# Two GpSimd additions of 128x2048 per feed-forward group, written as four of 128x512 each

## The chip, the cores and the metric

The kernel runs on one core of one Trainium2 chip. The metric is the device time of one launch in microseconds (us), the median over several runs. A core has five engines with queues of their own: PE (TensorE, matmuls), DVE (VectorE), ACT (ScalarE), POOL (GpSimd) and SP (SyncE, which here only issues transfers). They meet through semaphores and through tiles in the on-chip memory (SBUF) and in the accumulation banks of PE (PSUM).

## The reference

```python
def _L0_xattn_ref(embeds, patch_embeds, patch_lens, W_in, b_in, g_res, g_init):
    h = rmsnorm(embeds, g_res)
    h = jnp.einsum('bld,ed->ble', h, W_in) + b_in
    h_patch = rmsnorm(patch_embeds, g_init)
    return _hnet_depool(h, h_patch, patch_lens)   # a linear scan over the context, rows of it gathered, + h

def _L0_ffn_ref(x, w1, b1, w2, b2):
    h = jax.nn.gelu(jnp.einsum('bse,eh->bsh', x, w1) + b1, approximate=False)
    return jnp.einsum('bsh,he->bse', h, w2) + b2

x = x + _L0_xattn_ref(_layernorm(x, axis=-1), ctx_2048, mask_BxS2_if0, ...)
x = x + _L0_ffn_ref(_layernorm(x, axis=-1), L0_ffn_w1, L0_ffn_b1, L0_ffn_w2, L0_ffn_b2)
```

x is 4096 x 512 in float32, the context 3202 x 1024, the feed-forward layer 512 to 2048 to 512.

## The kernel before

There are two stages. The first (to about 185 us) takes x in 32 tiles of 128 rows: layer norm, projection by W_in, residual, and the result is stored to a DRAM buffer `x1_dram` (`x_part` in the profile). Beside it the context is scanned in blocks, and the scanned rows go to a DRAM table (`scan_table`).

The second stage is the feed-forward layer, in 8 groups of 512 rows, g = 0 to 7. A group is 16 steps m (`M`), each a slice of 128 hidden columns. Every float32 operand of a matmul is split into a high and a low part, so each product is three matmuls (`split_product`, L773 to L775). For each m:

- `ffn1(g, m)` on PE: 12 matmuls from `xt_hi`/`xt_lo` and the first weights into bank `h_bank[m % 2]`.
- ACT takes the gelu of it twice: `h_hi` (L734), rounded, and `g_f32` (L736), full. There is one `g_f32`, so L736 of step m waits until DVE has read that of step m - 1 (`h_split`).
- DVE makes `h_lo` as `g_f32 - h_hi` (L1134), both inputs in SBUF.
- `ffn2(g, m)` on PE: 12 matmuls from `h_hi`/`h_lo` and the second weights into the four banks `acc`. It waits for `h_lo` of its step.

PE's order within a group is ffn1(0), ffn1(1), ffn2(0), ffn1(2), ffn2(1), ... , ffn1(15), two transposes of the next group's rows, ffn2(14), the other two, ffn2(15). So at the start of a group two ffn1 stand one behind the other, with no ffn2 between ffn1(1) and the first ffn2 that needs an `h_lo` of this group. In groups 0 to 3 PE also does the scan's `carry`, three matmuls at m = 11.

What GpSimd does in a group is written out in its own `group(g, scan, prep)` (L574 on), in this order:

1. `x_cur = x_next + b2` (L579), one operation of 128x2048. It waits for the normalised rows (`n_b_ready`) and for the four stores of the previous group's output (`out_stored`), since `x_cur` is the buffer that is stored. `x_cur_ready` lets SP load the next group's rows to `x_next`.
2. Only in groups 0 to 3: `context_scale` and four `times_g_init` of 128x512 (L502) for the scan; in group 0 also four `low_weights` of 128x512 (L475).
3. `prepare(g + 1)` (L509): the gather's indices (L487), `x_next += b_in` (L491), one operation of 128x2048 in place, and then four gathers (L496), one per tile of 128x512, which add rows of the scan table to `x_next` by an indirect DMA. `step(...)` makes each operation end before the next one of the engine starts.
4. `group_scale(g + 1)` (L506, L507), which waits for DVE's statistics.

DVE waits for each tile's gather (`gathered[i]`) in `second_stats`: tiles 0 and 1 behind its step m = 11, tiles 2 and 3 behind m = 12. At the group's end it adds `acc` to `x_cur` tile by tile (L1158, waits for `x_cur_ready`), and SP stores each tile.

DVE's L1134 and its wait:

```python
dve.wait_ge(gelu_done, CREDIT + M * g + m + 1)
dve.wait_ge(h_used, NT + M * g + m - 1)
dve.tensor_tensor(h_lo[:, m % 2, :], g_f32[:], h_hi[:, m % 2, :].bitcast(F32),
                  ALU.subtract).then_inc(h_split, 1)
```

Of the kernel before, what the change touches and what calls it, by code (L numbers as in the profile page):

```python
# [22 lines left out]
ALU = mybir.AluOpType  # L23
# [7 lines left out]
P = 128  # L31
S, D, HID = 4096, 512, 2048
CTX, DG = 3202, 1024
TI = 4
# [13 lines left out]
NB = 7  # L48
NA = 3
# [4 lines left out]
STORED = 16  # L54
# [13 lines left out]
def wait_apart(engine, sem, value):  # L68

    engine.wait_ge(sem, value)  # L70
    engine.nop(nofuse=True)
# [24 lines left out]
def xattn_ffn(nc, x, ctx, mask, w_in, b_in, g_res, g_init, w1, b1, w2, b2, out):  # L96
# [11 lines left out]
    with es:  # L108
        def sb(name, shape, dt=F32):
            return es.enter_context(nc.sbuf_tensor(name, shape, dt))  # L110

        def sem(name):
            return es.enter_context(nc.semaphore(name))
# [8 lines left out]
        def place(name, shape, dt=F32, size=0, offset=None):  # L122
            where = at[0] if offset is None else offset
            t = nc.alloc_sbuf_tensor_at(name, shape, dt, offset=where)
            if offset is None:
                at[0] += size
            return t
# [12 lines left out]
        x_cur = place("x_cur", [P, TI, D], F32, 8 * KB)  # L140
        x_next_at = at[0]
        x_next = place("x_next", [P, TI, D], F32, 8 * KB)
# [32 lines left out]
        b_in_b = sb("b_in_b", [P, D])  # L175
        b2_b = sb("b2_b", [P, D])
# [64 lines left out]
        table_stored = sem("table_stored")  # L241
# [40 lines left out]
        x_cur_ready = sem("x_cur_ready")  # L282
# [147 lines left out]
        def _(pool):  # L430
            own = Tally(pool_self)

            def step(ins):
                wait_apart(pool, pool_self, own.inc(ins))
# [36 lines left out]
            def low_weights(c, q, high_ready, done):  # L471

                pool.wait_ge(w_hi_done, high_ready)
                r = slice(q * D, (q + 1) * D)
                pool.tensor_tensor(w_lo[:, c, r], w_raw[:, c, r], w_hi[:, c, r].bitcast(F32),  # L475
                                   ALU.subtract).then_inc(done, 1)

            def context_scale(b):
                pool.wait_ge(sq_done, R * b + R)
                step(pool.tensor_tensor(ss[:], ss_h[:], ss_l[:], ALU.add))  # L480
                step(pool.tensor_scalar(ss[:], ss[:], 1.0 / DG, RMS_EPS, ALU.mult, ALU.add))
                step(pool.tensor_tensor(rc[:], ss[:], neg_half[:], ALU.pow))
                pool.tensor_scalar(rc[:], rc[:], B_COEF, 1.0, ALU.mult, ALU.mult).then_inc(rc_ready, 1)

            def gather_indices(g):

                step(pool.tensor_copy(idx[:], plug[:, bass.ds(TI * g, TI)]))  # L487

            def add_bias(v, b):

                step(pool.tensor_tensor(v, v, b, ALU.add))  # L491

            def add_context(g, i, blocks):

                rows = table[0:STEP * blocks, :]
                pool.indirect_dma_start(x_next[:, i, :], None, rows, bass.IndirectOffsetOnAxis(  # L496
                    ap=idx[:, i:i + 1].bitcast(U32), axis=0), compute_op=ALU.add).then_inc(gathered[i], 16)

            def times_g_init(b, j):

                pool.wait_ge(sq_done, R * b + j + 1)
                pool.tensor_tensor(cl[:, j, :], cl[:, j, :], g_init_b[:], ALU.mult).then_inc(g_scaled, 1)  # L502

            def group_scale(g):
                wait_apart(pool, mv_b_ready, TI * (g + 1))
                step(pool.tensor_scalar(va_b[:], mv_b[:, :, 1], LN_EPS, 1.0, ALU.add, ALU.mult))  # L506
                pool.tensor_tensor(rb[:], va_b[:], neg_half[:], ALU.pow).then_inc(rb_ready, 1)  # L507

            def prepare(g, blocks):  # L509
                gather_indices(g)  # L510
                pool.wait_ge(x_next_loaded, 16 * (g + 1))
                add_bias(x_next[:], b_in_b[:].unsqueeze(1).to_broadcast([P, TI, D]))
                wait_apart(pool, table_stored, STORED + 16 * blocks)
                for i in range(TI):
                    add_context(g, i, blocks)

            def span(h, last=False):
# [56 lines left out]
            def group(g, scan, prep):  # L574

                pool.wait_ge(n_b_ready, TI * (g + 1))
                if not isinstance(g, int) or g > 0:
                    pool.wait_ge(out_stored, 16 * TI * g)
                pool.tensor_tensor(x_cur[:], x_next[:], b2_b[:].unsqueeze(1).to_broadcast([P, TI, D]),  # L579
                                   ALU.add).then_inc(x_cur_ready, 1)  # L580
                if scan:
                    context_scale(NA + g)
                    for j in range(R):
                        times_g_init(NA + g, j)
                if isinstance(g, int) and g == 0:
                    for q in range(4):
                        low_weights(7, q, 7, w2_ready)
                if prep:
                    prepare(g + 1, g + 3 if scan else NB)
                    group_scale(g + 1)  # L590

            for g in range(NB - NA):
                group(g, True, True)
            with pool.Fori(NB - NA, NG - 1) as g:
                own.looped(g, NB - NA, 1 + 1 + 1)
                group(g, False, True)
            own.left(NG - 1 - (NB - NA))
            group(NG - 1, False, False)


# [593 lines left out]
```

## Time and profile before

| | |
|---|---|
| median of 3 runs | 949.41 us |
| lowest and highest run | 947.39 and 951.27 us |
| profiled execution, span from first to last instruction | 946.3 us (the profile lists no other time for this execution) |
| PE busy | 863.1 us, 91% |
| DVE, ACT, POOL busy | 337.7, 293.1, 271.9 us |
| mean granted TensorE clock | 0.949 of full speed |
| share of PE in the chain that ended last | 77% |

The span is of one execution, the median of others. Start times in the rows below count from the span's start. A granted clock of 1.00 is TensorE's 2.4 GHz level, 0.50 its 1.2 GHz level; a window with a value between them held both.

### The profile page before, as it was taken

What the parts mean: (1) busy time and instruction counts of PE and PEld (TensorE: products, weight loads), DVE (VectorE), ACT (ScalarE), POOL (GpSimd) and SP (SyncE); (2) the same over time, 40 slices, a digit from 0 to 9 for tenths busy, and PEclk for the clock granted to TensorE, in tenths of its full rate; (3) what the DMA queues carried; (4) which work ended last, traced back from release to release, by engine and by line L of the source; (5) the groups of instructions that cost most, each with busy time, mean ns of one, the idle gap of its engine ahead of it and who ended that gap; (6) DMA issues with size and microseconds to landing.
All of it is one profiled execution on the core that took longest, in us unless ns stands there. A gap on an engine that the chain in (4) does not pass through costs nothing.

```text
span 946.3 us, 11247 instructions
## 1 busy us (share of the span) xinstructions
PE 863.1 (91%) x3781; PEld 705.7 (75%) x3781; DVE 337.7 (36%) x531; ACT 293.1 (31%) x505; POOL 271.9 (29%) x278
## 2 busy tenths in 40 slices
PE   5789786299999999899989998999899989998998
PEld 4567565178888887788868886888688868886886
DVE  4767566411452244224422442123212421242112
ACT  3465661133323422242324231222122222222221
POOL 4265455563601521043114306000600060001000
PEclk8899897689999999899999998999899989998999
DMA  7956655330314033203230223001300130000001
GB/s 224 290 176 227 226 179 144 90 136 23 45 63 147 11 48 111 95 11 44 101 108 11 44 87 81 10 1 45 79 10 0 43 77 13 0 30 15 1 1 44
DMA packets 34413, 73.13 MB, mean 77 GB/s; under 512 B 5548, under 2 KB 6572, under 8 KB 31984
## 3 DMA queue, kind: packets, MB, share of 16 engines
q1 hardware_dynamic: 25124, 57.34, 17.9%
q0 software_dynamic: 4608, 8.39, 5.9%
q10 hardware_dynamic: 4656, 7.09, 2.4%
q8 instruction: 13, 0.21, 0.1%
q14 instruction: 12, 0.10, 0.0%
HBM read 48.92 MB, written 23.89 MB: 77 GB/s over the span
## 4 chain that ended last, share of the span: by engine, by line
PE 77%; DMA 8%; DVE 7%; POOL 3%; issue 2%; ACT 1%; ACTq 1%; SPq 0%; POOLq 0%; DVEq 0%
PE acc L773 13%; PE acc L775 13%; PE acc L774 13%; PE h_bank L773 12%; PE h_bank L774 12%; PE h_bank L775 12%; DMA x_part<-xb 4%; DVE h_lo L1134 3%; PE t_bank L817 1%; DMA x_next<-scan_table,idx 1%; DMA x_next<-x_part 1%; DMA g_init_b<-in_L_xattn_g_init_dram 1%; DMA xa<-in_x_dram 1%; DVE h_lo L917 1%; POOL x_next L491 1%
## 5 line engine op out<-in xcount | busy, mean ns | idle before, releaser
L1134 DVE TENSOR_TENSOR h_lo<-g_f,h_hi 128x512 fp32r<-128x512 f32 x128 | 129.1, 1009 | 515.4 <-ACT g_f L736 507.1
L734 ACT ACTIVATE h_hi<-h_bank,b_c 128x512 fp32r<-128x512 f32 x128 | 88.3, 690 | 510.4 <-PE h_bank L775 510.4
L773 PE MATMUL acc<-w_hi,h_hi 128*128 128x512 f32 x512 | 206.7, 404 | 22.1 <-DVE h_lo L1134 22.1
L775 PE MATMUL acc<-w_hi,h_lo 128*128 128x512 f32 x512 | 204.7, 400 | 0.0
L774 PE MATMUL acc<-w_lo,h_hi 128*128 128x512 f32 x512 | 204.5, 399 | 0.0
L773 PE MATMUL h_bank<-xt_hi,w_hi 128*128 128x512 f32 x512 | 201.5, 394 | 1.5 <-DVE xt_lo L1058 1.5
L774 PE MATMUL h_bank<-xt_lo,w_hi 128*128 128x512 f32 x512 | 200.6, 392 | 0.0
L775 PE MATMUL h_bank<-xt_hi,w_lo 128*128 128x512 f32 x512 | 200.2, 391 | 0.0
L773 PEld LDWEIGHTS acc<-w_hi,h_hi 128*128 128x128 f32 x512 | 98.9, 193 | 45.4 <-issue 20.9
L775 PEld LDWEIGHTS acc<-w_hi,h_lo 128*128 128x128 f32 x512 | 99.2, 194 | 21.4
L773 PEld LDWEIGHTS h_bank<-xt_hi,w_hi 128*128 128x128 f32 x512 | 97.6, 191 | 22.5 <-ACT xt_hi L720 1.9
L774 PEld LDWEIGHTS acc<-w_lo,h_hi 128*128 128x128 f32 x512 | 99.4, 194 | 20.0
L774 PEld LDWEIGHTS h_bank<-xt_lo,w_hi 128*128 128x128 f32 x512 | 97.4, 190 | 20.5
L775 PEld LDWEIGHTS h_bank<-xt_hi,w_lo 128*128 128x128 f32 x512 | 97.1, 190 | 20.5
L736 ACT ACTIVATE g_f<-h_bank,b_c 128x512 f32<-128x512 f32 x128 | 87.3, 682 | 16.3 <-DVE h_lo L1134 16.3
L579 POOL TENSOR_TENSOR x_cur<-x_next,b_b 128x2048 f32<-128x2048 f32 x8 | 36.9, 4615 | 144.9 <-DMA out_dram<-x_cur 144.7
L773 PE MATMUL acc<-win_hi,h_hi 128*128 128x512 f32 x128 | 58.0, 453 | 13.3 <-DVE h_lo L917 13.3
L506 POOL TENSOR_SCALAR va_b<-mv_b 128x4 f32<-128x4 f32 x8 | 1.6, 197 | 216.5 <-DVE mv_b L1044 216.5
L496 POOL DMA_INDIRECT x_next<-scan_table,idx x32 | 53.6, 1674 | 15.5 <-POOL x_next L491 9.1
L775 PE MATMUL acc<-win_hi,h_lo 128*128 128x512 f32 x128 | 54.7, 427 | 0.0
L774 PE MATMUL acc<-win_lo,h_hi 128*128 128x512 f32 x128 | 54.4, 425 | 0.0
L491 POOL TENSOR_TENSOR x_next<-x_next,b_in_b 128x2048 f32<-128x2048 f32 (+1 forms) x11 | 38.0, 3452 | 21.6 <-DMA x_next<-x_part 21.0
(133 smaller groups left out, 686.5 us busy)
## 6 DMA issues: line engine op xcount, KB each, us to landing
xa<-in_x_dram SPq DMA_DIRECT2D x32, 256.0 KB, 5.8
x_part<-xb SPq DMA_DIRECT2D x32, 256.0 KB, 3.6
x_next<-x_part SPq DMA_DIRECT2D x8, 1024.0 KB, 5.1
out_dram<-x_cur SPq DMA_DIRECT2D x32, 256.0 KB, 2.1
w_raw<-in_L_ffn_w_dram ACTq DMA_DIRECT2D x6, 1024.0 KB, 11.0
cl<-in_ctx_dram SPq DMA_DIRECT2D x6, 1024.0 KB
ch<-in_ctx_dram SPq DMA_DIRECT2D x16, 256.0 KB, 2.7
scan_table<-cl SPq DMA_DIRECT2D x4, 992.0 KB
```

The source lines that it names most:

```text
L491: step(pool.tensor_tensor(v, v, b, ALU.add))
L496: pool.indirect_dma_start(x_next[:, i, :], None, rows, bass.IndirectOffsetOnAxis(ap=idx[:, i:i + 1].bitcast(U32), axis=0), compute_op=ALU. ...
L506: step(pool.tensor_scalar(va_b[:], mv_b[:, :, 1], LN_EPS, 1.0, ALU.add, ALU.mult))
L579: pool.tensor_tensor(x_cur[:], x_next[:], b2_b[:].unsqueeze(1).to_broadcast([P, TI, D]), ALU.add).then_inc(x_cur_ready, 1)
L734: act.activation(h_hi[:, m % 2, :], h_bank[m % 2][:], ACT.Gelu, bias=b1_c[:, m:m + 1])
L736: act.activation(g_f32[:], h_bank[m % 2][:], ACT.Gelu, bias=b1_c[:, m:m + 1]).then_inc(gelu_done, 1)
L773: nc.tensor.matmul(dst, a_hi, b_hi, start=first, stop=False)
L774: nc.tensor.matmul(dst, a_hi, b_lo, start=False, stop=False)
L775: return nc.tensor.matmul(dst, a_lo, b_hi, start=False, stop=final)
L817: ins = nc.tensor.transpose(t_bank[i % 2][:, k * P:(k + 1) * P], n_rows[:, i, k * P:(k + 1) * P], ident[:])
L917: dve.tensor_tensor(h_lo[:, t % 2, :], t_bank[t % 2][:], h_hi[:, t % 2, :].bitcast(F32), ALU.subtract).then_inc(t_lo, 1)
L1134: dve.tensor_tensor(h_lo[:, m % 2, :], g_f32[:], h_hi[:, m % 2, :].bitcast(F32), ALU.subtract).then_inc(h_split, 1)
```

## The change

Both 128x2048 additions of GpSimd's group are written as loops over the four tiles of 128x512. In `prepare` the gather of each tile now follows that tile's own piece of the addition; the wait for the scan table stands behind the first piece. The four pieces of `x_cur` follow one another with no wait between them, and the last one raises `x_cur_ready`. The count of the engine's own semaphore per loop turn goes from 3 to 6.

```diff
             def prepare(g, blocks):
                 gather_indices(g)
                 pool.wait_ge(x_next_loaded, 16 * (g + 1))
-                add_bias(x_next[:], b_in_b[:].unsqueeze(1).to_broadcast([P, TI, D]))
-                wait_apart(pool, table_stored, STORED + 16 * blocks)
                 for i in range(TI):
+                    add_bias(x_next[:, i, :], b_in_b[:])
+                    if i == 0:
+                        wait_apart(pool, table_stored, STORED + 16 * blocks)
                     add_context(g, i, blocks)
...
                 if not isinstance(g, int) or g > 0:
                     pool.wait_ge(out_stored, 16 * TI * g)
-                pool.tensor_tensor(x_cur[:], x_next[:], b2_b[:].unsqueeze(1).to_broadcast([P, TI, D]),
-                                   ALU.add).then_inc(x_cur_ready, 1)
+                for i in range(TI):
+                    ins = pool.tensor_tensor(x_cur[:, i, :], x_next[:, i, :], b2_b[:], ALU.add)
+                ins.then_inc(x_cur_ready, 1)
...
-                own.looped(g, NB - NA, 1 + 1 + 1)
+                own.looped(g, NB - NA, 1 + TI + 1)
```

GpSimd's order from group 0's `prepare` to the `x_cur` addition of group 1, with what each waits for, before:

```order
L487 COPY idx<-plug 128x4
L491 TENSOR_TENSOR x_next<-x_next,b_in_b 128x2048 [waits pool_self,x_next_loaded]
L496 DMA x_next<-scan_table,idx 128x512 [waits pool_self,table_stored]
L496 DMA x_next<-scan_table,idx 128x512 x3
L506 TENSOR_SCALAR va_b<-mv_b 128x4 [waits mv_b_ready]
L507 TENSOR_TENSOR rb<-va_b,neg_half 128x4 [waits pool_self]
L579 TENSOR_TENSOR x_cur<-x_next,b_b 128x2048 [waits out_stored,n_b_ready]
L480 TENSOR_TENSOR ss<-ss_h,ss_l 128x4 [waits sq_done]
```

The same place with the change (the `x_cur` addition is L581 there):

```order
L491 TENSOR_TENSOR x_next<-x_next,b_in_b 128x512 [waits pool_self,x_next_loaded]
L496 DMA x_next<-scan_table,idx 128x512 [waits pool_self,table_stored]
L491 TENSOR_TENSOR x_next<-x_next,b_in_b 128x512
L496 DMA x_next<-scan_table,idx 128x512 [waits pool_self]
...
L506 TENSOR_SCALAR va_b<-mv_b 128x4 [waits mv_b_ready]
L507 TENSOR_TENSOR rb<-va_b,neg_half 128x4 [waits pool_self]
L581 TENSOR_TENSOR x_cur<-x_next,b_b 128x512 [waits out_stored,n_b_ready]
L581 TENSOR_TENSOR x_cur<-x_next,b_b 128x512 x3
L480 TENSOR_TENSOR ss<-ss_h,ss_l 128x4 [waits sq_done]
```

Nothing else moved past the addition of `x_cur`: one operation became four with the waits in front of the first. In `prepare` the gathers of tiles 0 to 2 moved ahead of the later pieces of the addition, and each gather now waits for its piece. The other engines' orders are unchanged.

## Rows read from the trace of the kernel before

**Rows 1.** Page, 40 equal slices of the span, the granted TensorE clock in tenths.

```profile
PEclk8899897689999999899999998999899989998999
```

**Rows 2.** Page, the chain that ended last, shares of the span by engine.

```profile
PE 77%; DMA 8%; DVE 7%; POOL 3%; issue 2%; ACT 1%; ACTq 1%; SPq 0%; POOLq 0%; DVEq 0%
```

**Rows 3.** Page, costliest groups: busy and mean ns, then idle before and releaser.

```profile
L1134 DVE TENSOR_TENSOR h_lo<-g_f,h_hi 128x512 fp32r<-128x512 f32 x128 | 129.1, 1009 | 515.4 <-ACT g_f L736 507.1
```

**Rows 4.** Waits of PE from 190 us on: us in total, times, longest.

```profile
PE acc L773 <- DVE h_lo L1134: 22.1, 6, 3.8
```

**Rows 5.** Timeline of 374 to 383 us: start, duration, engine, line, operation, [idle before].

```profile
375.78 4.53 POOL L579 TENSOR_TENSOR x_cur<-x_next,b_b 128x2048 f32<-128x2048 f32 x1 [19.63 <-DMA out_dram<-x_cur]
...
376.06 4.79 DVE L1134 TENSOR_TENSOR h_lo<-g_f,h_hi 128x512 fp32r<-128x512 f32 x1 [3.06 <-ACT g_f L736]
...
376.66 0.39 PE L774 MATMUL h_bank<-xt_lo,w_hi 128*128 128x512 f32 x1
376.89 0.39 PE L775 MATMUL h_bank<-xt_hi,w_lo 128*128 128x512 f32 x1
381.10 0.77 PE L773 MATMUL acc<-w_hi,h_hi 128*128 128x512 f32 x1 [3.83 <-DVE h_lo L1134]
381.67 0.63 PE L774 MATMUL acc<-w_lo,h_hi 128*128 128x512 f32 x1
382.09 0.63 PE L775 MATMUL acc<-w_hi,h_lo 128*128 128x512 f32 x1
```

**Rows 6.** Windows of 4 us around it: busy per engine (count), granted clock, DMA, GB/s.

```profile
372.00:376.00 4.00, 4.00 (x20) 3.30 (x19) 1.01 (x2) 1.27 (x2) 0.22 (x1) 1.00 0.76 271
...
380.00:384.00 4.00, 2.90 (x7) 2.36 (x8) 1.55 (x2) 0.69 (x1) 0.31 (x1) 0.50 0.92 334
384.00:388.00 4.00, 4.00 (x14) 3.18 (x13) 0.00 (x0) 0.00 (x0) 0.00 (x0) 0.69 0.18 76
```

**Rows 7.** Chain that ended last: each group's first transposes of the next rows.

```profile
274.99 0.87 PE t_bank L817 x8
...
364.58 0.88 PE t_bank L817 x8
...
842.14 0.87 PE t_bank L817 x8
```

**Rows 8.** Timeline of 286 to 293 us, the one boundary without a PE wait.

```profile
287.00 4.63 POOL L579 TENSOR_TENSOR x_cur<-x_next,b_b 128x2048 f32<-128x2048 f32 x1 [20.43 <-DMA out_dram<-x_cur]
286.46 0.69 DVE L1134 TENSOR_TENSOR h_lo<-g_f,h_hi 128x512 fp32r<-128x512 f32 x1 [3.05 <-ACT g_f L736]
```

**Rows 9.** Timelines around 236 and 185 us: GpSimd's 128x512 pieces and L1134 among them.

```profile
235.76 2.54 POOL L475 TENSOR_TENSOR w_lo<-w_raw,w_hi 128x512 fp32r<-128x512 f32 x2
...
237.70 1.14 DVE L1134 TENSOR_TENSOR h_lo<-g_f,h_hi 128x512 fp32r<-128x512 f32 x1 [4.30 <-ACT g_f L736]
...
230.31 5.49 POOL L502 TENSOR_TENSOR cl<-cl,g_init_b 128x512 f32<-128x512 f32 x4
...
185.88 11.16 POOL L475 TENSOR_TENSOR w_lo<-w_raw,w_hi 128x512 fp32r<-128x512 f32 x9
```

**Rows 10.** PE in the first stage: a gap, and the window of 4 us around it.

```profile
81.78 0.50 PE L773 MATMUL acc<-win_hi,h_hi 128*128 128x512 f32 x1 [1.14 <-DVE h_lo L917]
...
80.00:84.00 4.00, 2.86 (x14) 2.24 (x15) 3.86 (x8) 1.75 (x5) 1.02 (x4) 1.00 0.59 130
```

**Rows 11.** Chain at 158 us, timelines of group 0, and the gathers' time to landing.

```profile
158.25 1.25 POOL x_next L491
...
161.91 1.34 POOL x_next L491
...
241.53 4.60 POOL L491 TENSOR_TENSOR x_next<-x_next,b_in_b 128x2048 f32<-128x2048 f32 x1
...
263.18 0.68 DVE L1043 BATCH_NORM_STATS2 st_b<-x_next 128x6 f32<-128x512 f32 x1
...
DMA to landing us min/median/max: 4.6/5.2/12.5
```

## Prediction, made before the changed kernel was run

> **What bounds the kernel now.** I read the page first, then the waits of PE, then the timeline of one group boundary. The chain that ended last is three quarters PE [rows 2], so time is gained only where PE stands still or runs slowly. PE's granted clock dips at regular distances all through the feed-forward stage [rows 1], about once per group. A steady matmul load should not do that, so something stops PE at each boundary. The mean of 1009 ns for DVE's L1134 [rows 3] is the second sign: undisturbed the operation takes 0.69 us [rows 8], so a few must be very long. PE's waits name the place: six waits, 22.1 us together, all for `h_lo` [rows 4].
>
> The timeline shows one of the six [rows 5]. GpSimd starts its 128x2048 addition at 375.78. DVE starts `h_lo` of the group's first step at 376.06, 0.28 us later, and ends at 380.85, which is 0.54 us after GpSimd's end at 380.31. DVE did not run slowly: it stood behind the other operation and then did its own. PE's last matmul of ffn1(1) started at 376.89; the next one starts at 381.10 after 3.83 us idle, 0.25 us behind the end of `h_lo`. Boundary 0 to 1 is the counterproof [rows 8]: there `h_lo` starts at 286.46, before GpSimd at 287.00, takes 0.69 us, and PE does not wait.
>
> The stall has a second price. PE's clock is 1.00 before it, 0.50 in the 4 us with and behind it, 0.69 in the next [rows 6]: the engine had been idle, the clock fell from its 2.4 GHz to its 1.2 GHz level, and the matmuls follow at a distance of 0.42 us instead of 0.23 [rows 5].
>
> **What a boundary costs in all.** From 274.99 to 364.58 is one group without a wait, 89.59 us [rows 7]. It contains the scan's three carry matmuls, 3 x 0.23 = 0.68 us, so a group without the scan should take 88.91. From 364.58 to 842.14 are five groups, two with and three without the scan: 477.56 us, against 2 x 89.59 + 3 x 88.91 = 445.91. The excess is 31.65 us, 6.33 per boundary. Six boundaries: 38.0 us. Of it 22.1 is the wait [rows 4] and 15.9 the slow clock, 2.65 per boundary; twelve matmuls 0.2 us later each give 2.4, which fits.
>
> **The change part by part.**
>
> *The addition to `x_cur`, four pieces.* What decides is whether DVE gets its turn between two pieces. The trace has the nearest case already: GpSimd's runs of 128x512 operations, L502 and L475 [rows 9]. Two pieces from 235.76 end at 238.30. L1134 starts among them at 237.70 and ends at 238.84, again 0.54 us behind the end of the piece that it met, while two further pieces stand behind. So DVE waits for one piece, not for the run. A piece takes 11.16 / 9 = 1.24 us in an almost free run. Bounds: 4.53 / 4 = 1.13 from below, 5.49 / 4 = 1.37 from above, where a DVE operation is in the run [rows 5, 9]. I take 1.24, the row of most pieces. At the boundary shown, `h_lo` then ends at 375.78 + 1.24 + 0.54 = 377.56 and PE starts 0.25 later, at 377.81, instead of 381.10: 3.29 us earlier. It still waits 3.83 - 3.29 = 0.54. Over six boundaries the wait goes from 22.1 to 22.1 - 6 x 3.29 = 2.4 us, gain 19.7; with 1.13 or 1.37 a piece it is 20.4 or 18.9. If a race is won as in boundary 0 to 1 the rest goes too.
>
> *The clock.* A gap of about half a microsecond stands in place of 3.8. The trace shows a longer gap that cost nothing: 1.14 us in front of 81.78, in a window where PE was busy 2.86 of 4 us; its clock is 1.00 [rows 10]. So I take the 15.9 us as gained in full, lower end of the gain 0.
>
> *The later steps of a boundary.* `h_lo` of the second step comes while pieces 3 and 4 run. It is late by one piece at most, 1.24 + 0.54 - 0.69 = 1.1 us. From there on an ffn2 stands between two ffn1, 12 x 0.23 = 2.7 us more room, so it costs nothing. If that cover were gone it would be 1.1 us per boundary. The four pieces with two DVE operations among them end about 4 x 1.24 + 0.9 = 5.9 us after the first start, 1.3 later than now. `x_cur_ready` is later by that. Behind it stand SP's load of `x_next` and, through it, the next group's gathers. DVE needs those only at step 11, eleven steps of 24 matmuls at 0.23 us, some 60 us on, and its own additions to `x_cur` come later still. GpSimd has 19.63 us of idle time in front of the next L579 [rows 5]. Nothing.
>
> *The addition to `x_next` and the gathers.* The whole now costs 4.60 us and four gathers behind it. The last group of the first stage already does it piece by piece: from piece to piece, gather in between, 161.91 - 158.25 = 3.66 us [rows 11]. In group 0, the tightest, that gives 241.53 + 4 x 3.66 = 256.2 for the last issue's end, and 5.2 us to landing: 261.4. DVE reads tiles 2 and 3 from 263.18 on, so the last tile has 1.8 us to spare, and the first ones land earlier than now. Nothing gained, since no PE wait is put down to a gather, and nothing lost; at the worst landing of 12.5 us it would be 268.7, 5.5 us late, less 3 us of room in front of ffn2: 2.5 us, once. The pieces also shorten L1134's delays in steps 8 and 9, which no PE wait shows now.
>
> **The sum.** 19.7 + 15.9 = 35.6 us. Against the profiled span that is 946.3 - 35.6 = 910.7. The median of the runs stands 3.1 above the span (949.4), part of it work outside the span and part the spread of 2 us each way; I carry the difference over: 949.4 - 35.6 = 913.8 us, 3.7% less.
>
> **Rivals.**
>
> *B, the clock falls all the same.* The short gap stays, and behind it the two halves of the work may still lose the fast level at some boundaries. Against it is [rows 10], for it that this is a gap of another place. Six boundaries falling: only 19.7 is gained, 949.4 - 19.7 = 929.7. Three of six: 913.8 + 3 x 2.65 = 921.8. The Trainium skill's page "TensorE: Matmul & The Clock Gate", under "A second HAM failure mode: psum-queue depth-cycling", says that frequent short idles between groups of matmuls can make the clock swing between its levels; by that rule the time would come out between these two.
>
> *C, DVE is shut out until the fourth piece ends.* The L475 and L502 pieces each raise a semaphore, while the first three of `x_cur` raise none and wait for none, so the run might leave no opening. Then the stall lasts for four pieces, 4 x 1.24 = 4.96 instead of 4.53 us, 0.43 more at six boundaries: 2.6 us, 952.0. At 1.37 a piece it is 5.48, 0.95 more each, 5.7 in all: 955.1. That is slower than before; it passes 0.5% (4.7 us, 0.79 per boundary) from 1.33 us a piece on. Against it: in rows 9 the openings come although the next piece is issued with no time between, the nine pieces being one unbroken 11.16 us. The Trainium skill's page "GPSIMD Engine Reference", under "Instruction dispatch", says that the engine's cores start the next instruction as soon as each has done its own share, with nothing to hold them together; taken literally, some core would always be in the memory and C would follow. The rows here speak against that for pieces with an increment and say nothing of those without.
>
> *D, the waits are not of this cause.* If the long L1134 came from something else that ends with the addition by chance, the time would stay at 949. Six ends 0.54 to 0.56 us behind GpSimd's end speak against it.
>
> **Chances.** Forecast 0.80. B 0.11 (partly or wholly). C 0.06, two thirds of it within 0.5%. D 0.03. A measurement of this kernel can tell about 0.5%, 4.7 us, from no change. Faster by more than that: forecast and B, 0.91, and slower 0.02 from C's upper half; the rest, 0.07, is within 0.5%. The forecast's own range is 909.4 (all 38.0 gained and a median 2 us lower, as the lowest run is) to 918.0 (pieces of 1.37, the late gather of 2.5 and a median 1 us higher: 913.8 + 0.8 + 2.5 + 1). To hold 8 in 10 the range takes in three of six clock falls, 921.8: 909.4 to 922.
>
> **What would show it.** In the changed profile: PE's waits for `h_lo` sum to some 2 to 3 us instead of 22.1, each under 0.7; the mean of L1134 falls from 1009 ns to about 0.75 us; the L581 pieces start 1.24 us apart, 0.45 more where a DVE operation got in; the `PEclk` line has nines throughout the last 32 slices with no regular dips, and the group's length is 89 to 90 us each time. If `h_lo` at the boundary still lasts over 4 us, C is right. If it is short and the clock still falls, B is. If a wait for a gather appears on DVE in group 0, the late landing was real.

## The result and the profile after

The changed kernel takes 911.92 us, median of four runs (909.85 to 914.23), against 948.4 us (943.1 to 951.27, four runs) for the kernel before: a ratio of 0.9616, 95% interval 0.9573 to 0.9659. The prediction was 913.8 us. The profiled execution spans 908.1 us.

First the clock, which dipped once per group in [rows 1], and the chain by engine ([rows 2] before), from the page:

```profile
PEclk9899898789999999999999999999999999999999
...
PE 80%; DMA 6%; DVE 5%; POOL 4%; issue 3%; ACT 1%; ACTq 1%; SPq 0%; POOLq 0%; DVEq 0%
```

The dips are gone from the ninth slice on. Lines have moved by two: L1136 is the `h_lo` that was L1134, L581 the addition to `x_cur`. The row that answers to [rows 3], and PE's waits from 190 us on ([rows 4]):

```profile
L1136 DVE TENSOR_TENSOR h_lo<-g_f,h_hi 128x512 fp32r<-128x512 f32 x128 | 112.4, 878 | 487.0 <-ACT g_f L738 487.0
...
PE acc L775 <- DVE h_lo L1136: 2.5, 6, 0.6
```

Still six waits, 2.5 us in place of 22.1. The boundary that [rows 5] showed looks like this now, in the timelines of GpSimd, DVE and PE from 371 us:

```profile
371.85 5.92 POOL L581 TENSOR_TENSOR x_cur<-x_next,b_b 128x512 f32<-128x512 f32 x4 [19.60 <-DMA out_dram<-x_cur]
...
372.15 1.54 DVE L1136 TENSOR_TENSOR h_lo<-g_f,h_hi 128x512 fp32r<-128x512 f32 x1 [3.08 <-ACT g_f L738]
374.87 1.75 DVE L1136 TENSOR_TENSOR h_lo<-g_f,h_hi 128x512 fp32r<-128x512 f32 x1 [1.18 <-ACT g_f L738]
...
373.94 0.47 PE L775 MATMUL acc<-w_hi,h_hi 128*128 128x512 f32 x1 [0.57 <-DVE h_lo L1136]
374.24 0.40 PE L776 MATMUL acc<-w_lo,h_hi 128*128 128x512 f32 x1
374.48 0.40 PE L777 MATMUL acc<-w_hi,h_lo 128*128 128x512 f32 x1
```

GpSimd is first again, by 0.30 us, but `h_lo` ends at 373.69 and not 4.8 us after it started. PE stands for 0.57 us and goes on at the distance of the 2.4 GHz level, 0.24 us. The next `h_lo`, 374.87, gets in a second time. The windows of 4 us around it, for [rows 6]:

```profile
372.00:376.00 4.00, 3.43 (x16) 2.53 (x15) 2.66 (x2) 1.30 (x3) 4.00 (x3) 1.00 0.86 263
376.00:380.00 4.00, 4.00 (x20) 3.29 (x19) 0.62 (x1) 0.23 (x1) 1.77 (x2) 1.00 0.58 176
```

**Where the time came from.** For all kernels here I read the starts of the first transposes at each group's end from the chain, as in [rows 7]. For the changed kernel:

```profile
271.11 0.88 PE t_bank L819 x8
...
360.67 0.87 PE t_bank L819 x8
...
451.06 0.88 PE t_bank L819 x8
...
541.45 0.87 PE t_bank L819 x8
...
631.05 0.88 PE t_bank L819 x8
```

Group lengths: 89.56 us without a wait, 90.39 and 90.39 with the scan, 89.60 without it, where the kernel before had 96.16, 95.27 and 95.29. From the first of these starts to the end of the span it is 946.3 - 274.99 = 671.3 before and 908.1 - 271.11 = 637.0 after. I call this the **stretch**. It lost 34.3 us. The other 3.9 us of the span's difference lie ahead of it. The change doesn't account for them, as far as the traces show: 2.6 us are in the first stage, which is the same in both kernels (its last transposes, those for group 0, started between 183.5 and 190.9 us over the 14 traces of this study), and 1.3 us are in group 0, which took 87.6 to 90.7 us, in two traces of one and the same kernel 87.59 and 90.68. Six of the traces have a wait for `h_lo` of 0.9 to 1.7 us in group 0, and what is said below of the stretch leaves it out. So the stretch is the measure for small effects, and the medians carry some 2 us of the spread ahead of it.

### The profile page after: what moved, and what is told of

It is laid out like the page before. It is cut to its first block, busy times and chain, and to the rows that moved or that the text cites. A ratio compares the mean times of both kernels' runs of the same rounds, so it can differ in the third digit from the quotient of the medians.

```text
span 908.1 us, 11322 instructions
## 1 busy us (share of the span) xinstructions
PE 848.3 (93%) x3781; PEld 695.9 (77%) x3781; DVE 326.7 (36%) x531; ACT 292.6 (32%) x505; POOL 285.3 (31%) x323
## 4 chain that ended last, share of the span: by engine, by line
PE 80%; DMA 6%; DVE 5%; POOL 4%; issue 3%; ACT 1%; ACTq 1%; SPq 0%; POOLq 0%; DVEq 0%
PE acc L775 14%; PE acc L777 14%; PE acc L776 14%; PE h_bank L775 12%; PE h_bank L777 12%; PE h_bank L776 12%; DMA x_part<-xb 2%; PE t_bank L819 2%; DMA x_next<-scan_table,idx 1%; DMA x_next<-x_part 1%; DVE h_lo L1136 1%; DMA g_init_b<-in_L_xattn_g_init_dram 1%; POOL ra L466 1%; DMA xa<-in_x_dram 1%; POOL cl L502 1%
## 5 line engine op out<-in xcount | busy, mean ns | idle before, releaser
L1136 DVE TENSOR_TENSOR h_lo<-g_f,h_hi 128x512 fp32r<-128x512 f32 x128 | 112.4, 878 | 487.0 <-ACT g_f L738 487.0
L775 PE MATMUL acc<-w_hi,h_hi 128*128 128x512 f32 x512 | 201.2, 393 | 2.5 <-DVE h_lo L1136 2.5
L777 PE MATMUL acc<-w_hi,h_lo 128*128 128x512 f32 x512 | 199.5, 390 | 0.0
L776 PE MATMUL acc<-w_lo,h_hi 128*128 128x512 f32 x512 | 199.3, 389 | 0.0
L775 PEld LDWEIGHTS acc<-w_hi,h_hi 128*128 128x128 f32 x512 | 96.1, 188 | 24.5 <-issue 4.6
L777 PEld LDWEIGHTS acc<-w_hi,h_lo 128*128 128x128 f32 x512 | 96.1, 188 | 20.2
L776 PEld LDWEIGHTS acc<-w_lo,h_hi 128*128 128x128 f32 x512 | 96.2, 188 | 19.4
L581 POOL TENSOR_TENSOR x_cur<-x_next,b_b 128x512 f32<-128x512 f32 x32 | 46.4, 1480 | 144.6 <-DMA out_dram<-x_cur 144.4
L491 POOL TENSOR_TENSOR x_next<-x_next,b_in_b 128x512 f32<-128x512 f32 x32 | 54.1, 1691 | 22.5 <-DMA x_next<-x_part 21.9
```

The costliest lines, as they stand in the source:

```text
L581: ins = pool.tensor_tensor(x_cur[:, i, :], x_next[:, i, :], b2_b[:], ALU.add)
L775: nc.tensor.matmul(dst, a_hi, b_hi, start=first, stop=False)
L776: nc.tensor.matmul(dst, a_hi, b_lo, start=False, stop=False)
L777: return nc.tensor.matmul(dst, a_lo, b_hi, start=False, stop=final)
```

## The experiments

**One part at a time.** The addition to `x_cur` in pieces, `x_next` whole:

```diff
-                pool.tensor_tensor(x_cur[:], x_next[:], b2_b[:].unsqueeze(1).to_broadcast([P, TI, D]),
-                                   ALU.add).then_inc(x_cur_ready, 1)
+                for i in range(TI):
+                    ins = pool.tensor_tensor(x_cur[:, i, :], x_next[:, i, :], b2_b[:], ALU.add)
+                ins.then_inc(x_cur_ready, 1)
```

> Only the addition to x_cur in four pieces, the one to x_next whole. Theory (DVE's h_lo at the group boundary stands behind GpSimd's x_cur addition; one piece instead of four): this part carries it all, so six PE waits of 2.4 to 2.6 us in all, no fall of the clock after 200 us, a median within 3 us of the changed kernel's 911.9. Rival (the interleaved gathers carry a part): 5 us or more above 912. Rival C (DVE shut out of a run without waits) is out already by the changed kernel's own trace.

Measured: 914.4 us (911.7 to 915.44), ratio 0.9669 (0.9632 to 0.9706) to 944.89 of the kernel before in these 13 runs. Stretch 913.7 - 276.56 = 637.1, the changed kernel's 637.0; the traced execution only reached it 5.5 us later. The waits from 190 us on are seven, 3.5 us; the seventh, 0.9 us, is in group 0, before the stretch. This part alone makes the whole gain at the boundaries.

The other part alone: the change's loop in `prepare`, with `x_cur` left whole.

> Only the addition to x_next in pieces with the gathers between, x_cur whole. Theory: the boundary stall stays, six waits of 22 us in all, the clock falls six times, median 948 +-3, the same as before. Rival (gathers that land earlier help): 5 us or more below before. A cost of the interleaving would show as 2 us or more above before and as new PE waits near step 9 or 12 of groups 0 to 3.

Measured: 939.97 us, ten runs, ratio 0.9951 (0.9924 to 0.9977). Not the same as before: 0.5% less, by 4.9 us, which is about what the rival had said, though not for its reason (no PE wait is put down to a gather). Its trace has five waits, 18.6 us, and a stretch of 663.1, 8.2 less than before. At five boundaries GpSimd is first and the waits are as they were, 3.6 to 3.8 us; at the last, 6 to 7, it is not:

```profile
850.57 5.12 POOL L580 TENSOR_TENSOR x_cur<-x_next,b_b 128x2048 f32<-128x2048 f32 x1 [22.17 <-DMA out_dram<-x_cur]
...
850.53 0.69 DVE L1135 TENSOR_TENSOR h_lo<-g_f,h_hi 128x512 fp32r<-128x512 f32 x1 [2.88 <-ACT g_f L737]
```

`h_lo` was first by 0.04 us, and there is no stall. I took it for luck and asked for a second trace of the same kernel.

> The kernel with only x_next in pieces once more, for its trace. In its first trace the boundary 6 to 7 had no PE wait: h_lo started 0.04 us ahead of GpSimd's x_cur. Theory (a race by hundredths of a microsecond that the landing of the last output store decides, won there by chance): the last boundary goes either way in a new execution, the five others wait 3.5 to 3.8 us. Rival (the pieces of x_next make that boundary safe): no wait there again, by the same 0.04 us.

```profile
852.87 5.12 POOL L580 TENSOR_TENSOR x_cur<-x_next,b_b 128x2048 f32<-128x2048 f32 x1 [22.17 <-DMA out_dram<-x_cur]
...
852.84 0.69 DVE L1135 TENSOR_TENSOR h_lo<-g_f,h_hi 128x512 fp32r<-128x512 f32 x1 [2.89 <-ACT g_f L737]
```

The run took 940.83 us, with a stretch of 662.9. Again by 0.03 us: my "by chance" is wrong, the order came out the same in both executions. In the trace of before GpSimd starts 0.28 us ahead there (853.18 against 853.46, 21.86 us of idle time in front of it instead of 22.17). The output's four stores are issued in both 4.47 us before `h_lo`, so `h_lo` keeps its distance to the stores and it is GpSimd's own start that comes 0.3 us later. This boundary is worth 104.16 - 97.58 = 6.6 us, from the last group's transposes to the end of the span. Why GpSimd starts later I don't know; in the changed kernel, with the same loop in `prepare`, it does not (821.05 against 821.36).

The other 1.7 us of the 8.2 lie in the clock. Two of the groups with a stall are shorter than before, in both traces: 95.27 and 95.25 us instead of 96.16, and 94.50 and 94.48 instead of 95.29, and the waits in them are the same. The clock fell there too, but it came back sooner. For the boundary of [rows 5], where the window of 384 to 388 us had 0.69 before, the kernel with the gathers interleaved has:

```profile
380.00:384.00 4.00, 4.00 (x12) 3.12 (x12) 0.69 (x1) 0.25 (x1) 0.00 (x0) 0.57 0.80 292
384.00:388.00 4.00, 4.00 (x19) 3.29 (x18) 0.00 (x0) 0.77 (x2) 0.00 (x0) 1.00 0.01 6
```

PE had restarted at 379.77 here and at 381.10 before. There is one trace of the kernel before, and in it too one boundary of six was of the cheaper kind, so whether the gathers brought this about stays open.

**Order instead of length.** Both additions whole as before, but behind the group's first `h_lo`:

```diff
                     pool.wait_ge(out_stored, 16 * TI * g)
+                    pool.wait_ge(h_split, ONE + M * g + 1)
```

> Both additions whole as before, but GpSimd waits for DVE's h_lo of the group's first step before it starts on x_cur. Theory: the length of the addition does not matter, only which of the two comes first; first h_lo of each group 0.69 us, no PE wait for it, clock 1.00; the second h_lo is held until about 0.55 us behind the addition's end, near the end of the 2.7 us of room it has, so 0 to 0.5 us of PE wait per boundary; median 908 to 913. Rival (the piece length is what helps, by leaving room for all of DVE): waits of 1 us and more for the second h_lo and a median of 918 or more.

Measured: 909.63 us (906.79 to 912.36), ratio 0.963 (0.9587 to 0.9673), stretch 632.9, no PE wait for `h_lo` at all, group lengths 89.56 to 89.59 and 88.88.

```profile
376.24 4.61 POOL L580 TENSOR_TENSOR x_cur<-x_next,b_b 128x2048 f32<-128x2048 f32 x1 [20.77 <-DVE h_lo L1135]
...
375.38 0.69 DVE L1135 TENSOR_TENSOR h_lo<-g_f,h_hi 128x512 fp32r<-128x512 f32 x1 [3.05 <-ACT g_f L737]
378.11 3.29 DVE L1135 TENSOR_TENSOR h_lo<-g_f,h_hi 128x512 fp32r<-128x512 f32 x1 [2.04 <-ACT g_f L737]
```

The second `h_lo` lasts 3.29 us, and PE doesn't wait for it. So an addition of this length does no harm by itself. What costs is that it comes just in front of the one `h_lo` of a group that has no room.

**Order and pieces.** The same wait in front of `x_cur` in pieces (`x_next` whole), and in front of the changed kernel:

> x_cur in four pieces that start only after the group's first h_lo, x_next whole. Theory: the last 2.5 us of PE waits go, nothing else changes; median 907 to 911, span about 2.5 us below that of x_cur in pieces alone once the first stage's own spread is taken off. Rival (the 2.5 us come back elsewhere, since something else is just behind): no PE wait for h_lo but group lengths of 89.5 and more without the scan instead of 88.9.

> Both additions in pieces, as in the changed kernel, and x_cur only after the group's first h_lo. Theory: no PE wait for h_lo left, group lengths 89.57 us with the scan and 88.88 without, 4 us less than the changed kernel from the first group's transposes to the end, median 907 to 910 - the same as with x_cur alone in pieces or whole behind h_lo. Rival (the interleaved gathers free or cost something of their own once the boundary is clean): group lengths that differ from those by 0.3 us or more.

Measured: 909.2 us (907.28 to 910.23), ratio 0.9627 (0.9593 to 0.9662), stretch 905.5 - 272.67 = 632.8; and 908.92 us (905.99 to 912.05), ratio 0.9604 (0.956 to 0.9649), stretch 910.3 - 277.44 = 632.9. Neither has a PE wait for `h_lo` in the stretch; the second has one of 1.6 us in group 0. All three kernels with the wait have the same stretch and the same two group lengths, 88.86 to 88.88 without the scan and 89.55 to 89.59 with it. They beat the changed kernel by 4.1 us in the stretch and by 2.3 to 3.0 in the median; the medians and the ratios to the kernel before, each with its own runs, do not separate them from it, so the 4.1 us rest on the traces. Once the order is right, pieces add nothing.

**The length of the piece.** `x_cur` in two halves of 128x1024, in 128x1536 and 128x512, and in eight of 128x256:

```diff
-                pool.tensor_tensor(x_cur[:], x_next[:], ...
+                ins = pool.tensor_tensor(x_cur[:, 0:2, :], x_next[:, 0:2, :], ...
+                ins = pool.tensor_tensor(x_cur[:, 2:4, :], x_next[:, 2:4, :], ...
```

> x_cur in two operations of 128x1024. A half takes about 2.3 us, so h_lo ends at 2.3 + 0.54 = 2.85 us behind the start, PE waits about 1.6 us at each of six boundaries, 9.6 us in all. If the clock holds through a gap of 1.6 us: group lengths without the scan of 90.5 us, time 918 to 922. If it falls: 93 us and 932 to 938.

> x_cur as 128x1536 and then 128x512. The first takes about 3.4 us, h_lo ends 3.95 us behind the start, PE waits about 2.75 us per boundary, 16.5 us in all. Theory: the gap alone sets what the clock does; somewhere between 0.6 us (never fell) and 3.7 us (fell six times of six) it begins to fall; with falls at some boundaries only the group lengths are of two kinds, 91.7 and 94.2 us. Rival (the clock falls by the DMA or DVE traffic at the boundary): falls as often here as in the changed kernel, none.

> x_cur in eight operations of 128x256. A piece takes 0.6 to 0.75 us. Theory (h_lo waits for the end of the piece that it meets, plus 0.55 us): h_lo is at most 1.3 us long, the PE waits vanish, group lengths without the scan of 88.9 us, time 2 to 3 us below four pieces. Rival (a fixed cost per piece eats it): pieces of 1 us or more, x_cur done 3 us later, the waits stay at 0.4 us.

Halves: 928.64 us, one run, above the 918 to 922 expected. The waits at the boundaries are 1.31 to 1.65 us, about the 1.6 expected, and the clock never fell in the stretch. What I had not seen coming is a second wait, 12 us behind the first, in three groups without the scan:

```profile
565.83 0.47 PE L776 MATMUL acc<-w_hi,h_hi 128*128 128x512 f32 x1 [1.56 <-DVE h_lo L1137]
578.10 0.50 PE L776 MATMUL acc<-w_hi,h_hi 128*128 128x512 f32 x1 [1.15 <-DVE h_lo L1137]
```

What stands in front of it is the other whole addition. GpSimd's `x_next` starts 0.10 us ahead of an `h_lo`, and that one, with 2.7 us of room, is late by 5.03 - 0.69 = 4.3 us:

```profile
572.92 4.58 POOL L491 TENSOR_TENSOR x_next<-x_next,b_in_b 128x2048 f32<-128x2048 f32 x1 [4.50 <-DMA x_next<-x_part]
...
573.02 5.03 DVE L1137 TENSOR_TENSOR h_lo<-g_f,h_hi 128x512 fp32r<-128x512 f32 x1 [4.65 <-ACT g_f L739]
```

Three and one: 939.9 us, one run; the six waits are 2.75, 2.74, 2.66, 2.55, 2.57 and 2.41 us. The clock fell to its lower level behind the first three and behind none of the others. PE's first matmul behind the second, third and fourth wait, 0.77 us long at the lower level and 0.47 at the higher:

```profile
480.78 0.77 PE L776 MATMUL acc<-w_hi,h_hi 128*128 128x512 f32 x1 [2.74 <-DVE h_lo L1137]
...
576.08 0.77 PE L776 MATMUL acc<-w_hi,h_hi 128*128 128x512 f32 x1 [2.66 <-DVE h_lo L1137]
...
669.14 0.47 PE L776 MATMUL acc<-w_hi,h_hi 128*128 128x512 f32 x1 [2.55 <-DVE h_lo L1137]
```

A group with a fall took 93.2 us without the scan, 94.2 and 95.4 with it; one without a fall about 92.

Eight pieces: 912.47 us, one run. `h_lo` at the boundary lasts 1.00 us, PE doesn't wait, and the stretch is 633.9. The eight take 6.50 us with two `h_lo` among them, 0.6 more than four. Group lengths are 88.96 to 89.09 without the scan: a little over the 88.88 of the kernels with the wait.

**Is it the `x_next` addition?** Halves of `x_cur` again, with the gathers interleaved:

> x_cur in halves, and x_next in four pieces with the gathers between. With x_cur in halves alone three of the groups without the scan had a second PE wait of 1.1 us, 12 us behind the first. Theory: that is the whole 128x2048 addition to x_next, which meets h_lo of step 2 or 3 there; in pieces it goes, so lengths without the scan of 90.7 instead of 92.0 us, PE waits 9 us in six. Rival (the gathers' or another operation's): the second waits stay.

921.92 us, one run, group lengths 90.60 to 90.72 without the scan instead of 91.99 to 92.11, and no second wait. So the `x_next` addition was the cause. This is what the second half of the change is good for: it makes harmless a collision that costs nothing with `x_cur` in four pieces, where the stretch is 637.1 us with `x_next` whole and 637.0 with it in pieces.

**What of the addition keeps DVE out.** A memset of `x_cur`, which reads nothing (this kernel leaves out the residual and b2), and a copy, which reads one input (it leaves out b2). In both, each of the two waits in front also has an empty instruction of its own; GpSimd's idle time there stays 19.6 us:

```diff
-                pool.tensor_tensor(x_cur[:], x_next[:], b2_b[:].unsqueeze(1).to_broadcast([P, TI, D]), ALU.add)...
+                pool.memset(x_cur[:], 0.0).then_inc(x_cur_ready, 1)
```

> In place of the x_cur addition a memset of x_cur to 0, 128x2048, which reads nothing (left out: the residual x and b2 of the result). It takes 1.8 us. If DVE's h_lo, two inputs in SBUF, is kept waiting by GpSimd's reads: it takes 0.69 us even while the memset runs, and PE doesn't wait. If any GpSimd operation on SBUF keeps it out: it ends 0.55 us behind the memset, 2 us long, PE waits about 1.1 us at six boundaries.

> In place of the x_cur addition a copy of x_next to x_cur, 128x2048, one input in SBUF (left out: b2 of the result). It takes 2.3 us. If any read of GpSimd keeps DVE's h_lo waiting: h_lo ends 0.55 us behind the copy's end, 2.5 us long, PE waits about 1.6 us per boundary as with the addition in halves, time 918 to 922. If only an operation with two inputs does: h_lo 0.69 us, no wait, 908 to 913 as with the memset.

With the memset, 913.11 us (one run), stretch 633.1, no PE wait in it, and at each boundary the same picture:

```profile
379.09 1.82 POOL L579 MEMSET x_cur<- 128x2048 f32 x1 [19.61 <-DMA out_dram<-x_cur]
...
379.39 0.69 DVE L1133 TENSOR_TENSOR h_lo<-g_f,h_hi 128x512 fp32r<-128x512 f32 x1 [3.05 <-ACT g_f L735]
```

`h_lo` runs its 0.69 us in the middle of the memset. With the copy, 914.79 us (one run), stretch 640.8:

```profile
372.98 1.89 POOL L579 COPY x_cur<-x_next 128x2048 f32<-128x2048 f32 x1 [19.58 <-DMA out_dram<-x_cur]
...
373.30 2.11 DVE L1133 TENSOR_TENSOR h_lo<-g_f,h_hi 128x512 fp32r<-128x512 f32 x1 [3.08 <-ACT g_f L735]
```

It ends at 375.41, 0.54 us behind the copy, and PE waits six times, 6.3 us. The copy is shorter than I had put it, 1.89 for 2.3 us, so the time is below the 918 to 922 expected. The memset is as long as the copy, 1.82 and 1.89 us, so the length doesn't tell them apart. One read of GpSimd is enough to hold a DVE operation with two SBUF inputs, and a write is not. The Trainium skill's page "SBUF — State Buffer" has this rule under "SBUF: two separate sides", where it tells of the port pair that the two engines share, an exclusive lock for a whole instruction that a DVE operation with two SBUF inputs contends for only against a GpSimd operation that reads SBUF. The runs with the addition, the copy and the memset agree.

## Why the prediction was right, point by point

*The cause.* Right: `h_lo` behind GpSimd's operation. The wait in front of the addition removed the stall with the operation left whole. The memset removed it in the same place and order, where the copy, as long but with one read, kept 6.3 us of it.

*DVE's turn between pieces.* Right, and rival C with it refuted: `h_lo` ends 1.84 us behind the first piece's start where 1.24 + 0.54 = 1.78 was expected, though these pieces have neither wait nor increment between them. C had supposed that GpSimd's cores run on from one piece into the next and so leave no opening; the opening was there. The third piece started 1.69 us behind the second, and not 1.25 like the second behind the first: about the 0.45 more that was forecast for a DVE operation in between. PE's waits are 2.5 us, 2.4 were predicted.

*The clock.* Right: no fall in the stretch, rival B refuted for gaps of 0.2 to 0.6 us. The study also shows that this term had room: the clock held through 1.67 us too.

*The size.* The sum said 35.6 us, the stretch lost 34.3. What was mis-sized is the price of the short gap that stays: I had counted only the wait. Against the floor of 88.88 us, a group with a 0.35 us wait takes 89.50, and against 89.58 one of 0.57 takes 90.39: 0.24 to 0.27 us more than the wait each time, 1.5 over six boundaries. It follows that the 15.9 us were not all the clock's: some 1.5 us of them go with the six gaps by this measure. That the median came within 1.9 us of the forecast is in part luck. The gain that missed in the stretch, 1.3 us, was made up by about 2 us of spread ahead of it, and the median of the kernel before came out 1.0 lower this time, 948.4 for 949.4. And the 3.1 us that I carried from the span to the median were too many: the run with the changed kernel's span of 908.1 took 909.85, so 1.75 lie outside the span.

*The cover of the later steps.* Right. The second `h_lo` takes 1.75 us, 1.06 late (1.1 said), and the four pieces 5.92 us (5.9 said), and no one waits.

*The gathers.* Right in that they cost and gave nothing at the end, wrong in their pace: 3.92 us from one to the next (239.80 to 251.57 for three) where 3.66 was said. And a cost was missed that lies off the path. DVE's scan rows of groups 0 to 3, which have two inputs in SBUF, now meet piece after piece, 3.98 to 4.24 us for three of them instead of 2.13 or 2.14. The first row is of before, the second of the changed kernel, both of group 0:

```profile
246.61 2.13 DVE L932 SCALAR_TENSOR_TENSOR cl<-cl 128x512 f32<-128x512 f32 x3
```

```profile
239.90 4.24 DVE L934 SCALAR_TENSOR_TENSOR cl<-cl 128x512 f32<-128x512 f32 x3
```

The mean of L1136 is 878 ns and not the 750 of the last paragraph of the prediction. That figure was too low by the prediction's own sum: two late `h_lo` at each of six boundaries, 0.85 and 1.06 us late, already bring it to about 780. The rest are the `h_lo` that meet a piece elsewhere, among them one of 1.85 to 2.33 us in each of the groups 1 to 6 at the pieces of `x_next`. No PE wait comes of them.

*The floor.* 88.91 us for a group without the scan was worked out from one group and three matmuls; the kernels with the wait show 88.88.

## What to carry to other kernels

When a DVE operation with two SBUF inputs shows a mean well above its minimum, look at what GpSimd does in front of each long one: it may be standing behind it. Here an operation of 0.69 us took up to 4.8, nearly all of the GpSimd instruction more. Two cures were shown to work, cutting the GpSimd operation to the length that the waiting chain can bear, and letting it wait for the one DVE operation that has no slack; the second takes one wait in the code and left no PE wait for `h_lo` in the stretch. If PE's stall is long enough for the clock to fall, count that too: here the clock and the restarts came to 15.9 us on top of 22.1.

## What the runs showed of the hardware that was not expected

- DVE's operation ended 0.54 to 0.56 us behind the end of the GpSimd operation that held it, whether that was a piece of 1.29 us, a copy of 1.89 us or an addition of 4.53 us, although it takes 0.69 us by itself.
- PE's clock never fell behind gaps of 0.2 to 1.67 us in the stretch, and it fell behind all sixteen of 3.5 to 3.8 us (six before, five in each trace with only the gathers interleaved). Of the six of 2.4 to 2.75 us it fell behind the three longest, 2.66 us and more, and behind none of 2.57 us and less; that is one execution, so it shows no threshold.
- Hundredths of a microsecond decide who is first and then 6.6 us: 0.04 and 0.03 us in the kernel with only the gathers interleaved, in two executions of two. What moved GpSimd's start by 0.3 us there, after the loop's last turn, stays open.
